# Attention and ternary feed-forward in one kernel: normalisations on GpSimd, head 0's row-max steps inside the token groups, biases as products with ones

## The chip, the cores and the metric

The kernel runs on one core of a Trainium2 chip. Its time is that of the device, in microseconds, as the median over the executions. The core has five engines with a queue each: TensorE (PE: matmuls and transposes, PEld its weight loads), VectorE (DVE), ScalarE (ACT), GpSimd (POOL) and SyncE (SP), which issues most of the DMAs. Each works through its instructions in their order and waits on semaphores.

## The reference

Input x is (2, 2048, 256): two sequences of 2048 tokens with 256 channels, all in float32. Cut to what matters:

```python
xn = (x - mean) / sqrt(var + 1e-5)
# attention: 16 heads of 16 channels, the keys are the queries
z = layernorm(xn) * g + b
q, v = z @ wq.T + bq, z @ wv.T + bv          # k = q
out = softmax(q @ q.T / 4) @ v                # per sequence and head
attn = out @ w_out.T + b_out
# feed-forward with ternary weights: clip(round(w / mean|w|), -1, 1)
h = gelu(xn @ ternary(W1).T + b1)             # 1024 wide
ffn = h @ ternary(W2).T + b2
return x + attn + ffn
```

## The kernel before

**Token groups.** The 4096 tokens are taken in NG = 8 groups of 512, groups 0 to 3 being the first sequence. For a group, VectorE takes the statistics (`stats_of`), GpSimd raises the variances to the power -1/2 (`rsqrt`), and VectorE writes two normalised copies, xn for the feed-forward and zn for the attention, in 8 instructions of 128x256 (`norm`). TensorE transposes both into four PSUM banks. ScalarE and VectorE split the transposed tiles into two float16 parts each (`second_parts`). TensorE then forms half of the values of the group before (`values`), its down projection (`ffn_down`: 64 products of 128x256 into `pf`), the queries of this group in three products of parts, and eight hidden blocks of 128 features. ScalarE applies GELU to each and writes the first float16 part, VectorE the second (`results`, 4 instructions of 128x1024). The down projection of a group thus lies in the TensorE stretch of the next one; that of group 7 comes last. The queries go to DRAM (`q_parts`), from where SyncE loads each head's keys and queries; head 0's are loaded during group 3, once the first sequence is stored.

**Scales.** Before group 0's queries, scales are found that keep the float16 parts in range. ScalarE takes absolute values, TensorE forms sums with them, VectorE adds the biases' part, takes the maximum and derives the scales (`sigma`); the weights are then scaled and split (`scaled`, and a subtraction on VectorE). `ternary` makes the ternary weights from W1 and W2 on VectorE, `out_scale` does for wo what `sigma` does for the others.

**Heads.** There are 32 heads (16 channels x 2 sequences). A head has 32 row-max steps, `a_step`: TensorE writes two products of 128x512 scores into a pair of PSUM banks, and VectorE reduces the 1024 columns to a maximum (`max_step`, L838). There are two such pairs, banks 0 to 3, so step a waits until step a - 2 has been reduced. The groups' transposes use the same four banks, and so wait for all steps given out so far. With a head's maxima complete (`split_max`), they are split into parts, transposed and put below the queries by DMA; then TensorE forms the scores again with the maximum taken off (`b_chunk`, L384), ScalarE takes the exponential (L1046), TensorE multiplies with the values (L367). Head h's exponentials run beside the row-max steps of head h + 1, which are 8 steps ahead (`AHEAD` 2 times `STEPS` 4).

**Order.** All queues are written out by hand. Of head 0's 32 steps, three lie in the hidden blocks of each of groups 4, 5 and 6, after blocks 1, 3 and 5 (`BETWEEN`). In group 7, six lie in the second half of group 6's down projection (`EARLY`) and seven in the hidden blocks. The other ten, and two of head 1, lie in group 7's own down projection. Six more of head 1 follow it, and then the exponentials of head 0 begin. A call `between` in `ffn_down` comes after each four products.

## Time and profile before

| | us |
|---|---|
| median of 3 runs (lowest, highest) | 1461.1 (1459.36, 1463.54) |
| profiled execution | 1464.5 |
| its span | 1462.7 |
| VectorE busy | 1351.0 (92%) |
| TensorE busy | 1396.9 (96%) |
| ScalarE busy | 1243.2 (85%) |
| GpSimd busy | 113.7 (8%) |
| first exponentials' product of head 0 starts at | 240.49 |

TensorE's matmuls are pipelined and their ends are modelled, so its busy time says less than that of the others. The span is that of one profiled execution; the median is over executions without a profile. PEclk is the clock granted to TensorE, as a share of 2.4 GHz. The program's numbers of buffers are left out of names: `w` is w1 or w2, whose buffers later hold the hidden parts and the probabilities; `weight_scratch` holds absolute and scaled weights.

### The profile page before, as it was taken

To read this page: it belongs to the slowest core of one execution; us is meant where nothing else is said; L and a number is where in the kernel's file an instruction comes from. 1 tells how busy PE (TensorE), PEld (TensorE's weight loads), DVE (VectorE), ACT (ScalarE), POOL (GpSimd) and SP (SyncE) were. 2 spreads that over 40 slices of the span, in tenths; PEclk is the share of its full clock that TensorE was granted. 3 is DMA by queue.
4 is the path that set the end of the run, shared out by engine and by line. 5 is a ranking of instruction groups with operands and counts; after the bars stand their busy time and mean duration, and the time that the engine had idled before them with its cause. 6 is when DMAs were issued, how large, how long until landed. Compare 5 with 4: busy or idle time off the path is not lost.

```text
span 1462.7 us, 31753 instructions
## 1 busy us (share of the span) xinstructions
PE 1396.9 (96%) x13166; PEld 445.3 (30%) x13166; DVE 1351.0 (92%) x1430; ACT 1243.2 (85%) x2284; POOL 113.7 (8%) x246
## 2 busy tenths in 40 slices
PE   6899988999999999999999999999999999999999
PEld 4666542222222222222222222222222222222244
DVE  7767789999999999999999999999999999999944
ACT  5564543999999999999999999899999999999975
POOL 2000006000000000000000000000111100001100
PEclk8999998999999999999999999999999999999999
DMA  5012000000000000000000001001212100011122
GB/s 228 15 40 69 30 15 1 28 30 29 29 30 29 30 30 29 26 26 29 29 30 29 30 29 34 30 31 34 59 59 59 59 30 32 31 32 59 38 92 86
DMA packets 28529, 60.65 MB, mean 41 GB/s; under 512 B 6200, under 2 KB 11736, under 8 KB 28130
## 3 DMA queue, kind: packets, MB, share of 16 engines
q1 hardware_dynamic: 27810, 56.99, 11.5%
q8 instruction: 103, 1.69, 0.5%
q10 hardware_dynamic: 576, 1.65, 0.3%
q14 instruction: 40, 0.33, 0.1%
HBM read 41.29 MB, written 16.77 MB: 40 GB/s over the span
## 4 chain that ended last, share of the span: by engine, by line
DVE 54%; PE 37%; ACT 5%; issue 3%; DMA 2%; POOL 0%; SPq 0%; ACTq 0%; DVEq 0%
DVE part_max L838 50%; PE ps L367 13%; PE ps L384 8%; PE ps L330 5%; PE ps L1067 3%; ACT w L1046 3%; PE ps L1136 2%; PE ps L1082 2%; DVE w L830 1%; PE ps L458 1%; ACT w L1017 1%; DMA rows<-in_rows 1%; PE ps L439 1%; PE ps L1108 1%; ACT hidden L1012 1%
## 5 line engine op out<-in xcount | busy, mean ns | idle before, releaser
L838 DVE TENSOR_REDUCE part_max<-ps 128x1 f32<-128x1024 f32 x1024 | 1171.5, 1216 | 16.8 <-PE ps L330 13.8
L1046 ACT ACTIVATE w<-ps 128x512 f32<-128x512 f32 x2048 | 1104.5, 596 | 86.5 <-PE ps L384 50.6
L367 PE MATMUL ps<-w,v_ones 128*32 128x256 f32 (+1 forms) x7440 | 623.8, 407 | 0.4
L384 PE MATMUL ps<-qry,key 50*128 50x512 f16 x1984 | 424.1, 389 | 21.2 <-ACT w L1046 20.7
L330 PE MATMUL ps<-qry,key 48*128 48x512 f16 x2048 | 412.6, 381 | 15.1 <-DVE part_max L838 11.7
L367 PEld LDWEIGHTS ps<-w,v_ones 128*32 128x32 f32 x7440 | 146.6, 108 | 371.1 <-issue 206.8
L384 PEld LDWEIGHTS ps<-qry,key 50*128 50x128 f16 x1984 | 103.9, 93 | 475.3 <-ACT w L1046 443.2
L330 PEld LDWEIGHTS ps<-qry,key 48*128 48x128 f16 x2048 | 102.2, 95 | 46.1 <-DVE part_max L838 33.1
L637 POOL COPY v_ones<-v_all 128x128 f32<-128x128 f32 x64 | 18.6, 291 | 805.8 <-PE ps L367 805.8
L1067 PE MATMUL ps<-w_ternary,w 128*128 128x256 f16 x512 | 62.1, 278 | 6.2 <-DVE w L830 6.2
L1008 ACT ACTIVATE q_split<-ps,sigma_bq 128x512 f16<-128x512 f32 x16 | 11.0, 687 | 66.2 <-PE ps L1082 66.2
L830 DVE SCALAR_TENSOR_TENSOR w<-hidden,hidden_scale,w 128x1024 f16<-128x1024 f32 x32 | 40.9, 1282 | 25.6 <-ACT w L1017 25.5
L1136 PE MATMUL ps<-x,w_ternary 128*128 128x512 f16 x256 | 61.2, 381 | 0.0
L1067 PEld LDWEIGHTS ps<-w_ternary,w 128*128 128x128 f16 x512 | 49.2, 100 | 17.8 <-DVE w L830 7.5
L1012 ACT ACTIVATE hidden<-ps,columns 128x512 f32<-128x512 f32 x64 | 42.2, 680 | 9.5 <-PE ps L1136 8.1
L914 DVE SCALAR_TENSOR_TENSOR resid<-ps,y_unscale,resid 128x512 f32<-128x512 f32 x16 | 11.8, 744 | 30.7 <-PE ps L458 30.6
L1017 ACT ACTIVATE w<-hidden,hidden_scale 128x1024 f16<-128x1024 f32 x32 | 36.7, 1148 | 1.1
L1136 PEld LDWEIGHTS ps<-x,w_ternary 128*128 128x128 f16 x256 | 22.9, 98 | 31.8 <-issue 5.9
L644 POOL TENSOR_TENSOR max_split<-neg_max,shift_unit 128x16 f16<-128x16 f32 x32 | 7.1, 221 | 299.8 <-DVE neg_max L843 299.8
L1082 PE MATMUL ps<-z,wq_parts 128*128 128x512 f16 x96 | 24.6, 411 | 4.9 <-DVE wq_parts L851 4.9
L1082 PE MATMUL ps<-wv_parts,z 128*128 128x256 f16 x192 | 25.2, 285 | 0.0
L1028 ACT ACTIVATE o_evacuated<-ps 128x512 f32<-128x512 f32 x31 | 18.5, 597 | 7.6 <-PE ps L367 7.6
(144 smaller groups left out, 462.4 us busy)
## 6 DMA issues: line engine op xcount, KB each, us to landing
key<-q_parts SPq DMA_DIRECT2D x64, 128.0 KB
qry<-q_parts SPq DMA_DIRECT2D x64, 128.0 KB
o_heads<-o_evacuated SPq DMA_DIRECT2D x31, 256.0 KB, 10.2
resid<-in_x SPq DMA_DIRECT2D x8, 512.0 KB, 13.9
q_parts<-q_split SPq DMA_DIRECT2D x16, 256.0 KB, 2.5
key<-q_parts SPq DMA_DIRECT2D x64, 64.0 KB
qry<-q_parts SPq DMA_DIRECT2D x64, 64.0 KB
out<-resid SPq DMA_DIRECT2D x7, 512.0 KB, 3.6
```

The source lines that it names most:

```text
L330: mm = eng.matmul(pair[:, j * BANK:(j + 1) * BANK], key[v][r:r + ROWS, blk * P:(blk + 1) * P], qry[v][r:r + ROWS, c * BANK:(c + 1) * BANK] ...
L367: mm = eng.matmul(pv[32 * c:32 * c + 2 * D, c0:c1], vst[:, kb, :], prob[kb % 2][:, c * BANK + c0:c * BANK + c1], start=(kb == 0), stop=(kb ...
L384: eng.matmul(ring_bank(v, i, False), key[v][r:r + KROWS, kb * P:(kb + 1) * P], qry[v][r:r + KROWS, c * BANK:(c + 1) * BANK], start=True, s ...
L637: pool.tensor_copy(vst[:, k0:k0 + NBLK // 2, 0:D], v_all[:, ds(b * NBLK + k0, NBLK // 2), ds(hh * D, D)]).then_inc(s_vs, 1)
L830: dve.scalar_tensor_tensor(out=hp[1][:, 2 * i:2 * i + 2, :], in0=hid[:, 2 * i:2 * i + 2, :], scalar=hs[:, 0:1], in1=hp[0][:, 2 * i:2 * i + ...
L838: dve.tensor_reduce(part_max[:, a // 2, a % 2:a % 2 + 1], pa[a % 2], AX.X, ALU.max).then_inc(s_r, 1)
L1012: act.activation(hid[:, f, :], pf[f % 2], ACT.Gelu, scale=1.0 / XS, bias=b1_col[:, f:f + 1]).then_inc(s_g, 1)
L1017: act.activation(hp[0][:, f - 1:f + 1, :], hid[:, f - 1:f + 1, :], ACT.Identity, scale=hs[:, 0:1]).then_inc(s_h1, 1)
L1046: act.activation(prob[kb % 2][:, c * BANK:(c + 1) * BANK], ring_bank(k, i, last), ACT.Exp, scale=exp_scale).then_inc(s_e, 1)
L1067: mm = pe.matmul(pf[t // 2][:, (t % 2) * C:(t % 2 + 1) * C], hp[i][:, f, t * P:(t + 1) * P], w2t[:, f, :], start=(f == 0 and i == 0), stop ...
L1082: mm = pe.matmul(out, rows(k, i, j), cols(k, i, j), start=(m == 0), stop=(m == len(terms) - 1))
L1136: mm = pe.matmul(pf[f % 2], w1t[:, k, f * P:(f + 1) * P], part[:, k, :], start=(k == 0 and i == 0), stop=(k == KC - 1 and i == 1))
```

## The change

- **Norms.** `norm` is a function of the engine now. Group 0's stays on VectorE; those of groups 1 to 7 go to GpSimd, each behind its power. A semaphore of its own (`normed`) tells TensorE, and VectorE, which must not overwrite the means before the norm has read them.
- **GpSimd** also takes the second parts of wq and wv and the float16 cast of the identity; its bias row moves behind the norms.
- **Biases.** bq and bv are loaded as one row on one partition, ahead of w1, instead of with the others on 128 partitions behind it. Their part of the sums comes from three products with a row of ones.
- **wo.** Its absolute values and sum move from group 0 to group 1, its scales to group 1, its scaling on ScalarE to group 2, its second part on VectorE to group 3.
- **Row-max steps.** Five are added in each down projection that lies in groups 4, 5 and 6; six lie in that of group 7's stretch, over three quarters of it, and six in its hidden blocks. All 32 of head 0 and four of head 1 have then been given out. The last four of the eight lie in group 7's own down projection (`REST`), and none follow it. The transpose of head 0's maxima comes ahead of that projection.
- Eight products with ones are added behind group 0's transposes, and an exponential of one column ahead of head 0's, which loads the table.

The diff, cut to its core:

```diff
...
+        row1 = sb("bq_bv", [1, 2 * C])
+        rabs = sb("bq_abs_bv_abs", [1, 2 * C])
...
+        DOWN = 5
+        DOWN_LAST = 6
+        PER_GROUP = DOWN + len(BETWEEN)
+        BEFORE_LAST = (NG - 1 - NG // NB) * PER_GROUP
+        IN_LAST = DOWN_LAST + KF - 2
+        REST = NA + STEPS * AHEAD - BEFORE_LAST - IN_LAST
...
+        def norm(eng, g):
+            x = resid[:, g * TG:(g + 1) * TG, :]
+            wait(eng, s_tr, g)
+            for n, dst in enumerate((xn, zn)):
+                for t in range(TG):
+                    last = eng.tensor_scalar(dst[:, t, :], x[:, t, :], mv[:, t, 0:1], rstd[:, n, t:t + 1],
+                                             ALU.subtract, ALU.mult)
+            last.then_inc(s_nm, 1)
...
+            load_x(1)
             sp.dma_start(w2[:, :], w_2).then_inc(s_w[1], 16)
-            load_x(1)
...
             rsqrt(0)
-            pool.wait_ge(s_row, 16)
-            pool.tensor_tensor(bias_row[:, :], bo_row, b2_row, ALU.add).then_inc(s_row, 1)
+            pool.wait_ge(s_id, 16)
+            pool.tensor_copy(idh[:, :], idf[:, :]).then_inc(s_idh, 1)
+            pool.wait_ge(s_wqs, KC + 1)
+            pool.tensor_tensor(wqp[:, 1, :, :], wqs, wqp[:, 0, :, :], ALU.subtract).then_inc(s_wqp, 1)
+            pool.wait_ge(s_wvs, KC + 1)
+            pool.tensor_tensor(wvp[:, 1, :, :], wvs, wvp[:, 0, :, :], ALU.subtract).then_inc(s_wvp, 1)
             for g in range(1, NG):
                 rsqrt(g)
+                pool.wait_ge(s_rs, g + 1)
+                norm(pool, g)
+            pool.wait_ge(s_out_b, 16)
+            pool.tensor_tensor(bias_row[:, :], bo_row, b2_row, ALU.add).then_inc(s_br, 1)
...
+                wait(dve, s_nm, g)
...
-                dve.wait_ge(s_abs, 3)
-                dve.tensor_tensor(vbound_row[:, :], bound_v, bv_abs[:, :], ALU.add)
-                dve.tensor_tensor(bound_row[:, :], bound_q, bq_abs[:, :], ALU.add).then_inc(s_sg, 1)
+                dve.tensor_reduce(bound[:, 0:2], bound_qv, AX.X, ALU.max)
+                dve.tensor_scalar(bound[:, 2:3], sum_b1, float(C), None, ALU.add).then_inc(s_sg, 1)
...
-                    last = dve.tensor_scalar(bv2[:, j, :], bv_sum[:, :], vsc[:, 0:1], None, ALU.mult)
+                    last = dve.tensor_scalar(bv2[:, j, :], b_wv, vsc[:, 0:1], None, ALU.mult)
...
+                    if g == 1 and i == 2:
+                        out_scale()
...
-            norm(0)
+            dve.wait_ge(s_rs, 1)
+            norm(dve, 0)
             sigma()
             second_parts(0)
-            dve.wait_ge(s_wqs, KC + 1)
-            dve.tensor_tensor(wqp[:, 1, :, :], wqs, wqp[:, 0, :, :], ALU.subtract).then_inc(s_wqp, 1)
             ternary(0, w1, w1t)
             stats_of(1)
-            dve.wait_ge(s_wvs, KC + 1)
-            dve.tensor_tensor(wvp[:, 1, :, :], wvs, wvp[:, 0, :, :], ALU.subtract).then_inc(s_wvp, 1)
             q_split(0)
-            norm(1)
-            dve.wait_ge(s_id, 16)
-            dve.tensor_copy(idh[:, :], idf[:, :]).then_inc(s_idh, 1)
             ternary(1, w2, w2t)
-            out_scale()
             results(0)
-            steps = iter([(0, a) for a in range(NA)] + [(1, a) for a in range(2)])
+            steps = iter([(0, a) for a in range(NA)] + [(1, a) for a in range(STEPS * AHEAD)])
...
-                if g == 1:
+                if g == 3:
                     dve.wait_ge(s_ow, KC + 1)
                     dve.tensor_tensor(wop[:, 1, :, :], wos, wop[:, 0, :, :], ALU.subtract).then_inc(s_op, 1)
-                norm(g + 1)
-                for j in range(2):
-                    add_ffn(g - 1, j)
+                add_ffn(g - 1, 0)
+                if g >= NG // NB:
+                    first_rows(DOWN)
+                add_ffn(g - 1, 1)
                 q_split(g)
                 results(g, first_rows if g >= NG // NB else None)
             g = NG - 1
             second_parts(g)
             value(g - 1, 1)
             add_ffn(g - 1, 0)
-            first_rows(EARLY)
+            first_rows(DOWN_LAST)
             add_ffn(g - 1, 1)
             q_split(g)
             results(g, first_rows)
             value(g, 1)
-            first = EARLY + 2 * (KF // 2 - 1) + (NG - 1 - NG // NB) * len(BETWEEN)
-            first_rows(TG * KF // 4)
-            add_ffn(g, 0)
-            first_rows(NA - first - TG * KF // 4)
-            split_max(0)
-            first_rows(2)
-            add_ffn(g, 1)
+            first_rows(REST)
+            for j in range(2):
+                add_ffn(g, j)
             for h in range(1, NH):
-                for a in range(2 if h == 1 else 0, NA):
+                for a in range(STEPS * AHEAD if h == 1 else 0, NA):
...
+            act.dma_start(row1[:, :], rows[:, 0:2 * C]).then_inc(s_row, 16)
...
+            act.activation(rabs[:, :], row1[:, :], ACT.Abs).then_inc(s_abs, 1)
...
-                    act.wait_ge(s_wo, 16)
-                    act.activation(abso, wo[:, :, :], ACT.Abs).then_inc(s_oa, 1)
                 else:
                     if g == 1:
+                        act.wait_ge(s_wo, 16)
+                        act.activation(abso, wo[:, :, :], ACT.Abs).then_inc(s_oa, 1)
+                    if g == 2:
...
-                pe.wait_ge(s_ln, 4 * g + 4)
+                pe.wait_ge(s_nm, g + 1)
...
                 if g == 1:
                     pe.wait_ge(s_wd, 5)
+                if g == 2:
                     pe.wait_ge(s_od, 1)
-                wait(pe, s_r, max(0, g - NG // NB) * len(BETWEEN))
+                wait(pe, s_r, max(0, g - NG // NB) * PER_GROUP)
...
                     abs_total(0)
+                    warm(WARM // 2)
...
-                        ffn_down(g - 1, t, between_down if t >= TG // 2 else None)
+                        ffn_down(g - 1, t, between_down if t else None)
...
                         abs_total(1)
+                    if g == 1 and f == 1:
                         pe.wait_ge(s_oa, 1)
...
-                    if between and (f in BETWEEN or (g == NG - 1 and f > 1)):
+                    if between and (f > 1 if g == NG - 1 else f in BETWEEN):
...
-            for out, rows, cols in ((bound_q, reach_rep, absq), (bound_v, reach_rep, absv), (b_wv, b_rep, wv)):
+            for out, left, right, bias in ((bound_qv[:, 0, :], reach_rep, absq, rabs[:, 0:C]), (bound_qv[:, 1, :], reach_rep, absv, rabs[:, C:2 * C]),
+                                           (b_wv, b_rep, wv, row1[:, C:2 * C])):
                 for k in range(KC):
-                    pe.matmul(out, rows[:, k, :], cols[:, k, :], start=(k == 0), stop=(k == KC - 1))
+                    pe.matmul(out, left[:, k, :], right[:, k, :], start=(k == 0), stop=False)
+                pe.matmul(out, ones[0:1, :], bias, start=False, stop=True)
...
-            def first_a_early(calls=iter(range(TG * KF // 4))):
-                n = next(calls)
-                if n == 0:
-                    pe.wait_ge(s_z, KC * NG)
-                    pe.wait_ge(s_x2, KC * NG)
-                if n < EARLY:
-                    first_a()
-            for g in range(1, NG - 1):
+            def in_down(g, count):
+                calls = iter(range((TG - 1) * KF // 2))
+                def call():
+                    n = next(calls)
+                    if n == 0:
+                        pe.wait_ge(s_z, KC * (g + 1))
+                        pe.wait_ge(s_x2, KC * (g + 1))
+                    if n % 2 == 0 and n >= (TG - 1) * KF // 2 - 2 * count:
+                        first_a()
+                return call
+            for g in range(1, NG):
+                if g < NG // NB:
+                    group(g)
+                    continue
                 if g == NG // NB:
                     pe.wait_ge(s_pad, 16 * (2 * ROT - 1))
-                group(g, first_a if g >= NG // NB else None)
-            group(NG - 1, first_a, first_a_early)
+                group(g, first_a, in_down(g, DOWN if g < NG - 1 else DOWN_LAST))
+            pe.wait_ge(s_idh, 1)
+            pe.wait_ge(s_vd, 2 * NG - 1)
...
+            max_transpose(pe, 0, 0)
             values(NG - 1, 1)
             pe.wait_ge(s_h2, KF // 2 * NG)
+            rest = iter(range(TG * KF // 2))
+            def rest_a():
+                n = next(rest)
+                if n % 2 and n // 2 < REST:
+                    first_a()
             for t in range(TG):
-                ffn_down(NG - 1, t, first_a)
-            pe.wait_ge(s_idh, 1)
+                ffn_down(NG - 1, t, rest_a)
             pe.wait_ge(s_vd, 2 * NG)
-            max_transpose(pe, 0, 0)
-            for a in range(2, STEPS * AHEAD):
-                a_step(pe, 1, 1, a)
...
```

TensorE in group 5, from the down projection that lies in it to the queries and on. Lines 330 and 333 are the row-max products, 1067 and 1071 the down projection, 1082 and 1086 queries and values, 1136 and 1142 the hidden blocks. Before:

```order
L1067 MATMUL ps<-w_ternary,w 128x256 x64
L1082 MATMUL ps<-z,wq_parts 128x512 x12
L1136 MATMUL ps<-x,w_ternary 128x512 x8
L330 MATMUL ps<-qry,key 128x512 x2
L1136 MATMUL ps<-x,w_ternary 128x512 x8
```

Changed:

```order
L1071 MATMUL ps<-w_ternary,w 128x256 x28
L333 MATMUL ps<-qry,key 128x512 x2
L1071 MATMUL ps<-w_ternary,w 128x256 x8
L333 MATMUL ps<-qry,key 128x512 x2
L1071 MATMUL ps<-w_ternary,w 128x256 x8
L333 MATMUL ps<-qry,key 128x512 x2
L1071 MATMUL ps<-w_ternary,w 128x256 x8
L333 MATMUL ps<-qry,key 128x512 x2
L1071 MATMUL ps<-w_ternary,w 128x256 x8
L333 MATMUL ps<-qry,key 128x512 x2
L1071 MATMUL ps<-w_ternary,w 128x256 x4
L1086 MATMUL ps<-z,wq_parts 128x512 x12
```

The row of 64 products is opened five times for a row-max step; the queries behind it, and the three steps in the hidden blocks, stand as before.

TensorE again, from the values ahead of group 7's own down projection to head 0 (line 351 and 354: the transpose of the maxima; 384 and 387: the exponentials' scores). Before, its beginning (two of twelve steps) and its end:

```order
L1082 MATMUL ps<-wv_parts,z 128x256 x12
L1067 MATMUL ps<-w_ternary,w 128x256 x4
L330 MATMUL ps<-qry,key 128x512 x2
L1067 MATMUL ps<-w_ternary,w 128x256 x4
L330 MATMUL ps<-qry,key 128x512 x2
L1067 MATMUL ps<-w_ternary,w 128x256 x4
```

```order
L1067 MATMUL ps<-w_ternary,w 128x256 x4
L330 MATMUL ps<-qry,key 128x512 x2
L1067 MATMUL ps<-w_ternary,w 128x256 x16
L351 MATMUL ps<-ident_f,max_split 32x128
L330 MATMUL ps<-qry,key 128x512 x12
L384 MATMUL ps<-qry,key 128x512 x2
L330 MATMUL ps<-qry,key 128x512 x2
```

Changed, the whole of it:

```order
L354 MATMUL ps<-ident_f,max_split 32x128
L1086 MATMUL ps<-wv_parts,z 128x256 x12
L1071 MATMUL ps<-w_ternary,w 128x256 x8
L333 MATMUL ps<-qry,key 128x512 x2
L1071 MATMUL ps<-w_ternary,w 128x256 x8
L333 MATMUL ps<-qry,key 128x512 x2
L1071 MATMUL ps<-w_ternary,w 128x256 x8
L333 MATMUL ps<-qry,key 128x512 x2
L1071 MATMUL ps<-w_ternary,w 128x256 x8
L333 MATMUL ps<-qry,key 128x512 x2
L1071 MATMUL ps<-w_ternary,w 128x256 x32
L387 MATMUL ps<-qry,key 128x512 x2
```

Eight of twelve steps have left the projection, and the six that stood behind the transpose are gone.

GpSimd, behind its first constants, with what each waits for. Before:

```order
L620 TENSOR_TENSOR rstd<-var_eps,minus_half 128x8 [waits ln_dve]
L624 TENSOR_TENSOR bias_row<-rows 128x256 [waits rows_loaded]
L620 TENSOR_TENSOR rstd<-var_eps,minus_half 128x8 [waits ln_dve] x7
L637 COPY v_ones<-v_all 128x8x16 [waits v_done]
L637 COPY v_ones<-v_all 128x8x16
L644 TENSOR_TENSOR max_split<-neg_max,shift_unit 128x16 [waits max_dve]
```

Changed, to the second norm:

```order
L633 TENSOR_TENSOR rstd<-var_eps,minus_half 128x8 [waits ln_dve]
L637 CAST ident_f<-ident_f 128x128 [waits ident_loaded]
L639 TENSOR_TENSOR wq_parts<-weight_scratch,wq_parts 128x512 [waits wq_scaled]
L641 TENSOR_TENSOR wv_parts<-weight_scratch,wv_parts 128x512 [waits wv_scaled]
L633 TENSOR_TENSOR rstd<-var_eps,minus_half 128x8 [waits ln_dve]
L500 TENSOR_SCALAR xn<-resid,mean_var,rstd 128x256 [waits transposed,ln_pool]
L500 TENSOR_SCALAR xn<-resid,mean_var,rstd 128x256 x3
L500 TENSOR_SCALAR zn<-resid,mean_var,rstd 128x256 x4
L633 TENSOR_TENSOR rstd<-var_eps,minus_half 128x8 [waits ln_dve]
L500 TENSOR_SCALAR xn<-resid,mean_var,rstd 128x256 [waits transposed,ln_pool]
L500 TENSOR_SCALAR xn<-resid,mean_var,rstd 128x256 x3
```

Each later power now stands behind the norm of the group before, and the staging of head 0's values behind all seven norms.

## Rows read from the trace of the kernel before

**Rows 1.** The page: span, and the costliest group of lines (busy, mean ns, idle before).

```profile
span 1462.7 us, 31753 instructions
...
L838 DVE TENSOR_REDUCE part_max<-ps 128x1 f32<-128x1024 f32 x1024 | 1171.5, 1216 | 16.8 <-PE ps L330 13.8
```

**Rows 2.** Stages: window, length, PE, PEld, DVE, ACT, POOL busy, PEclk, DMA share, GB/s.

```profile
44.00:53.00 9.00, 8.88 (x65) 7.23 (x66) 8.29 (x27) 0.00 (x0) 1.64 (x1) 0.81 0.01 2
68.00:112.00 44.00, 42.59 (x297) 28.50 (x296) 31.80 (x67) 25.58 (x37) 3.27 (x2) 1.00 0.12 39
219.00:241.00 22.00, 15.47 (x101) 6.84 (x99) 21.93 (x22) 1.55 (x2) 8.38 (x15) 0.97 0.00 1
241.00:254.00 13.00, 12.90 (x72) 2.28 (x70) 9.66 (x10) 8.00 (x15) 13.00 (x20) 0.52 0.01 1
```

**Rows 3.** Timeline of the start: start, length, engine, line, shapes, idle before.

```profile
12.18 1.07 PE L1108 MATMUL ps<-ident_f,xn 128*128 128x128 f32 x8
...
15.34 0.42 DVE L776 TENSOR_TENSOR v_bound_row<-ps,bv_abs 128x256 f32<-128x256 f32 x1 [3.57 <-ACT bq_abs L973]
...
17.03 1.06 ACT L986 ACTIVATE x<-ps 128x512 f16<-128x512 f32 x2
...
22.44 5.30 PE L1082 MATMUL ps<-z,wq_parts 128*128 128x512 f16 x12 [4.88 <-DVE wq_parts L851]
...
28.92 0.69 ACT L1012 ACTIVATE hidden<-ps,columns 128x512 f32<-128x512 f32 x1 [0.46 <-PE ps L1136]
...
38.60 3.68 DVE L830 SCALAR_TENSOR_TENSOR w<-hidden,hidden_scale,w 128x1024 f16<-128x1024 f32 x3
...
38.69 1.15 ACT L1017 ACTIVATE w<-hidden,hidden_scale 128x1024 f16<-128x1024 f32 x1
```

**Rows 4.** Chain of waits: start and length of five down projections on TensorE.

```profile
44.12 8.83 PE ps L1067 x64
...
67.80 7.16 PE ps L1067 x64
...
89.86 7.16 PE ps L1067 x64
...
138.50 6.99 PE ps L1067 x64
...
164.85 6.99 PE ps L1067 x64
```

**Rows 5.** Timeline of TensorE in group 4, of VectorE in group 5.

```profile
123.40 0.39 PE L330 MATMUL ps<-qry,key 48*128 48x512 f16 x2
...
133.59 1.58 PE L1108 MATMUL ps<-ident_f,xn 128*128 128x128 f32 x8 [2.35 <-DVE part_max L838]
...
142.37 0.68 DVE L752 TENSOR_TENSOR v_all<-ps,scaled_bv 128x512 f32<-128x512 f32 x1
```

**Rows 6.** GpSimd: timeline of two instructions, then groups of lines.

```profile
28.49 2.02 POOL L620 TENSOR_TENSOR rstd<-var_eps,minus_half 128x8 f32<-128x8 f32 x1 [13.22 <-DVE var_eps L714]
...
48.55 1.64 POOL L620 TENSOR_TENSOR rstd<-var_eps,minus_half 128x8 f32<-128x8 f32 x1 [18.03 <-DVE var_eps L714]
...
L631 POOL TENSOR_TENSOR resid<-resid,bias_row 128x256 f32<-128x256 f32 x32 | 21.9, 725 | 0.0
...
L664 POOL TENSOR_TENSOR hidden<-below_half,hidden 128x512 f16<-128x512 f32 x8 | 9.3, 1159 | 0.6
L662 POOL CAST hidden<-below_half 128x512 f16<-128x512 f32 x8 | 4.9, 609 | 0.5
```

**Rows 7.** Timeline of the last group and of the way into head 0.

```profile
193.40 0.39 PE L330 MATMUL ps<-qry,key 48*128 48x512 f16 x2
...
194.26 0.39 PE L330 MATMUL ps<-qry,key 48*128 48x512 f16 x2
...
218.59 0.61 PE L1067 MATMUL ps<-w_ternary,w 128*128 128x256 f16 x4 [1.12 <-DVE w L830]
...
235.43 11.40 DVE L838 TENSOR_REDUCE part_max<-ps 128x1 f32<-128x1024 f32 x10
```

99 lines of the change are left out of this document (43 added, 56 removed).

## The prediction

> **What bounds the kernel now.** I read the page first, then the table of stages, then the chain of waits with the timeline beside it for the first 275 us. The page [rows 1] gives VectorE's row-max reduction 1171.5 us of a span of 1462.7 us, with 16.8 us of idle time before its 1024 instructions: once the heads run, VectorE sets the pace. The change leaves a head alone, so it can only act ahead of a fixed point in head 0. I take the ninth row-max step of head 1. Both kernels have 40 steps behind them there, and everything after it is the same on every engine. VectorE's ten reductions from 235.43 begin with the third step of head 1 and take 1.14 each, so the ninth begins at 235.43 + 6 x 1.13 = 242.2 us [rows 7].
>
> Ahead of it lie eight token groups. In the plain groups TensorE is busy 42.59 of 44 us [rows 2], and one down projection follows the other after 89.86 - 67.80 = 22.06 us [rows 4]: TensorE, then ScalarE's last GELUs and VectorE's last hidden part. Groups 4 to 6 carry three row-max steps each and take 164.85 - 138.50 = 26.35 [rows 4]. From the last group's down projection on, VectorE is full (21.93 of 22 us) and TensorE waits for it (15.47) [rows 2].
>
> The sum is made against the profiled execution: 1464.5 us, span 1462.7. The median of the runs is 1461.1, and I put the difference on it.
>
> **The start, down to group 0's down projection (at 44.12).** VectorE's sigma chain begins at 15.34 after 3.57 of idle, behind two absolute values whose bias rows come in behind w1 [rows 3]. The small load now goes ahead of w1, and the three added products with ones run ahead of the transposes. The sums ended as the transposes began, at 12.18 [rows 3]; three more of 256 float32 columns cost about 0.5 each by their neighbours' pace, and the new absolute value of 512 columns delays them by about 0.5. So the sums end at 14.1, the transposes at 16.1, and ScalarE's copies start at 16.2, not 17.03 [rows 3]: 0.8 earlier. The first float16 part of wq then comes 0.8 earlier, GpSimd's subtraction (1.16 for this form) stands where VectorE's 0.68 stood, but VectorE's was queued behind its x and z parts. GpSimd's ends at about 20.9, so the q products start 1.5 ahead of their 22.44 [rows 3, 6], and the first GELU at 27.4 instead of 28.92.
>
> ScalarE needs from there to 38.69 + 1.15 = 39.84, that is 10.9 [rows 3]; without the wo product between the second and third hidden block, 0.6 less. Its last part is there at 37.7. Before, VectorE was late, not ScalarE: it took up the first three hidden parts only at 38.60 [rows 3]. The change takes from its queue ahead of them eight normalisations, two subtractions, a cast, the out-scale steps and a wait for GpSimd, some 7 us together. Now it needs 1.3 after ScalarE's last, and the down projection starts at 39.1: **-5.0**. The three cover each other: if only VectorE's queue improved, ScalarE's chain would still hold it at 41.2, which is -2.9. TensorE has no 2.9 us hole ahead of it any more, so the projection takes 7.16 rather than 8.83 [rows 4] at the granted clock of 0.81 there [rows 2]: **-1.7** (bounds -1.7 and 0). In group 1 the wo product (1.1 on TensorE) lies between hidden blocks where ScalarE has about 0.2 to spare: **+0.9**. The scale steps and casts of wo, moved to groups 1 to 3, lie in VectorE's and ScalarE's waits for TensorE: 0.
>
> **Norms on GpSimd.** No row shows this form there. Nearest are the two-input 128x256 addition at 725 ns and the one-input 128x512 cast at 609 ns [rows 6], so I take 0.5 each, 4 us for eight, between 0.3 and 1.3. In a plain group statistics end 4 us into the period, the power takes 1.64 [rows 6], and the transposes wait 18 us in: hidden up to 1.5 us each. In group 0 there are about 7 us for the eight, hidden up to 0.85 each. That VectorE is relieved of 2.8 us in a plain group is worth 0, because TensorE and ScalarE set the 22.06.
>
> **Five more steps in each down projection of groups 4 to 6.** A step costs TensorE 194.26 - 193.40 = 0.86 less the 0.45 of four projection products, so about 0.42 [rows 7]. Five are 2.1. VectorE must end the parts, the statistics and the values of the group (142.37 + 0.68, that is 4.55 after the projection's start at 138.50 [rows 4, 5]) and one residual addition before its first reduction, which ends at 6.35; the third step waits for that where it would have gone at 5.8. So 0.6 is lost, and 2.7 a group: **+8.1** for three (bounds 6.3, no stall, and 12). The steps inside the hidden blocks keep their order, and with it TensorE's 2.35 us wait before each group's transposes [rows 5]. The very first step is 3.1 us into group 3's projection (115.1) and needs head 0's queries and keys; before, it came at 123.40 and did not wait for them [rows 5]. Their loads are issued from 104 on: **+1.0**, between 0 and 8.3.
>
> **The last group and the way into head 0.** Six steps were in its second half before and are spread now: +0.8 for a stall on the third; the head's final maximum now falls in VectorE's full stretch: +0.2. Together **+1.0**. Group 7's own down projection starts at 218.59 [rows 7], and here the gain is. It holds four steps instead of twelve, and six outside are gone. TensorE needs 7.16 + 4 x 0.42 = 8.85; VectorE, at 1.13 a step, is not late. Two residual additions close it, the second at 228.3; the exponentials' products start, and the ninth step of head 1 comes two products and a step later, at 229.2 instead of 242.2: **-13.0** (bounds -11.5 and -13.6). The max rows' transpose and load, now ahead of the projection, are covered by it.
>
> **The clock in head 0.** From 241 to 254 the granted clock was 0.52, the low level of 1.2 GHz, and VectorE worked 9.66 of 13.0 us [rows 2]. It fell after TensorE had waited through five steps for VectorE at the end of the last group. That stretch is gone; TensorE now works 8.85 us through just before. I take **-3.0**, between 0 and the 3.3 that VectorE stood idle.
>
> **Contention.** GpSimd's power took 2.02 us beside a VectorE subtraction of two SBUF tensors, and 1.64 elsewhere [rows 6]. Its norms of group 1 now run beside VectorE's ternary steps, its bias additions (32 of 725 ns, 22 us, no longer beside row maxima alone) beside the hidden parts of group 7: **+1.0**, between 0 and 5. The Trainium skill, "SBUF — State Buffer", the reading of its diagram, has a rule against this change: the pair of ports that VectorE and GpSimd share is an exclusive lock for a whole instruction, taken by VectorE operations in a two-port mode or with two SBUF inputs. By that rule alone each meeting costs up to a whole instruction; the 0.38 us of the power agrees in direction.
>
> **Sum.** -5.0 - 1.7 + 0.9 + 8.1 + 1.0 + 1.0 - 13.0 - 3.0 + 1.0 = -10.7 us. 1461.1 - 10.7 = **1450.4 us**.
>
> **Rivals.**
> *A, half of it* (GpSimd and VectorE hinder each other). In group 0 eight norms of 0.5 and five VectorE instructions of 1.3 to 2.35 us take turns, so the norms end near 40 rather than 33, and the first projection at 42: +3. In group 7 three hidden parts wait up to 0.7 each: +2 over all. With the middle of the last term taken back: 1461.1 - 10.7 + 4 = 1454.4. For it speaks the 2.02; against it the reductions beside 22 us of GpSimd additions, still 1.13. This is where the skill's lock leads, worked out from these rows.
> *B, the clock stays low* in head 0 and after group 0: 3.0 + 1.7 come back, 1455.1. For it: TensorE still waits 2.35 in groups 4 to 6 and again for the two additions.
> *C, slower*: GpSimd's norm becomes the bound of every group. The place is the transposes' wait for the normed tiles. It decides from 1.5 us an instruction; each 0.1 more costs at most 0.8 in six groups, 4.8 in all, and the 10.7 are used up at 1.75: at 2.0 us, 1461.1 - 10.7 + 24 = 1474. Against it: the worst elementwise row there, with twice the columns, is below 1.3. The skill's "GPSIMD Engine Reference", section "Engine selection", advises VectorE for elementwise work and calls GpSimd about two times slower with two inputs, roughly line rate with one; that would leave it far from 1.5.
> *D, head 0's loads are late*: the first step stalls by 6 and TensorE's clock drops: 1450.4 + 6 = 1456.5.
> *E, the steps ride free*: no stall in the projections, no contention, full clock: 1446.
>
> **Chances.** Forecast 0.45, A 0.18, B 0.13, D 0.06, E 0.13, C and what I did not see 0.05. Runs spread by about 0.15% to either side, so 0.3% (4.4 us) is about what can be told from no change. The range takes the forecast, A, B and E: 1443 to 1457. Faster by over 4.4 us means below 1456.7: 0.86, with part of D beyond it; same 0.09; slower 0.05.
>
> **What would show it.** The first down projection near 39 and 7.2 long; the distance between down projections of groups 4 to 6 near 29; the first step of head 0 without a wait above 2; a granted clock of 1.0 over the 13 us after the exponentials begin, which begin near 233 (240.5 before); and heads of the same length as before. It is wrong if the transposes of any group wait for GpSimd, or if the heads themselves change.

## The result, and the profile after

| us | before | after |
|---|---|---|
| median of 7 runs (lowest, highest) | 1461.1 (1457.36, 1463.54) | 1471.31 (1467.09, 1473.16) |
| profiled execution, its span | 1464.5, 1462.7 | 1471.57, 1469.7 |

The ratio is 1.0066, 95% interval 1.0049 to 1.0084: slower by two thirds of a per cent, where 1450.4 us was forecast, between 1443 and 1457. Runs of one kernel lie 5 to 15 us apart where there are seven or more, and the higher the mean granted clock of a run, the shorter it is (1467.42 us at 0.991, 1471.57 at 0.986). Medians are compared below, and profiled executions only stage by stage. The medians are 10.2 us apart and the profiled executions 7.0: that of the kernel before lies 3.4 above its own median.

Everything behind the heads' start is as before. The page of the changed kernel answers to [rows 1]:

```profile
span 1469.7 us, 31804 instructions
...
L846 DVE TENSOR_REDUCE part_max<-ps 128x1 f32<-128x1024 f32 x1024 | 1171.6, 1213 | 18.5 <-PE ps L333 15.2
```

So the 7 us arose ahead of head 1's exponentials. The table sets the starts of the down projections on TensorE beside each other. The last row is head 1's final maximum, which both kernels reach with the same work behind them and some 1189.6 us ahead.

| | before | after | difference | this interval | forecast |
|---|---|---|---|---|---|
| group 0's projection | 44.12 | 50.01 | +5.9 | +5.9 | -5.0 |
| group 1's | 67.80 | 72.72 | +4.9 | -1.0 | -0.8 |
| group 3's | 111.93 | 116.74 | +4.8 | 0 | 0 |
| group 4's | 138.34 | 152.54 | +14.2 | +9.4 | +3.7 |
| group 5's | 164.65 | 180.17 | +15.5 | +1.3 | +2.7 |
| group 6's | 189.37 | 209.46 | +20.1 | +4.6 | +2.7 |
| group 7's | 218.59 | 241.40 | +22.8 | +2.7 | +1.0 |
| head 1's final maximum | 273.19 | 280.01 | +6.8 | -16.0 | -16.0 |

The windows of the changed kernel that answer to [rows 2], with one on the first row-max steps and one behind the exponentials' start (columns as there):

```profile
44.00:53.00 9.00, 7.86 (x56) 7.31 (x57) 3.44 (x7) 2.69 (x5) 1.09 (x1) 0.73 0.00 0
68.00:112.00 44.00, 42.55 (x298) 28.73 (x296) 28.85 (x55) 27.13 (x40) 23.23 (x18) 1.00 0.09 28
120.00:134.00 14.00, 9.73 (x52) 4.95 (x51) 8.16 (x16) 0.00 (x0) 11.32 (x9) 0.76 0.19 65
219.00:241.00 22.00, 17.61 (x94) 8.18 (x93) 17.72 (x18) 12.88 (x17) 10.03 (x13) 0.90 0.08 26
251.00:264.00 13.00, 11.65 (x106) 2.84 (x108) 12.04 (x11) 10.86 (x21) 5.38 (x8) 1.00 0.01 1
```

In the plain groups TensorE is as full as it was, though GpSimd now works 23 us in 44. From 44 to 53 it is not: its transposes begin only at 45.14. The chain of waits of the changed kernel says why (start, length, what; [rows 4] began with the same projection at 44.12):

```profile
29.11 1.65 POOL rstd L633
30.77 0.09 issue
30.86 8.82 POOL xn L500 x4
39.68 5.42 POOL zn L500 x4
45.10 0.04 issue
45.14 3.68 PE ps L1113 x16
48.82 1.36 PE ps L1086 x12
50.18 6.99 PE ps L1071 x64
```

Eight normalisations of group 1 take 14.24 us on GpSimd. The timeline of VectorE in the same stretch (start, length, line, shapes, idle before) shows that it had its hidden parts done by 40.4, 9.6 us before the projection, and what it ran beside the norms:

```profile
30.70 1.29 DVE L713 TENSOR_SCALAR below_half<-w,nhalf 128x2048 f32<-128x2048 f32 x1
32.02 2.53 DVE L715 SCALAR_TENSOR_TENSOR w_ternary<-w,half,below_half 128x2048 f16<-128x2048 f32 x1
34.65 3.93 DVE L838 SCALAR_TENSOR_TENSOR w<-hidden,hidden_scale,w 128x1024 f16<-128x1024 f32 x3
38.51 0.68 DVE L764 TENSOR_TENSOR v_all<-ps,scaled_bv 128x512 f32<-128x512 f32 x1
39.11 1.27 DVE L838 SCALAR_TENSOR_TENSOR w<-hidden,hidden_scale,w 128x1024 f16<-128x1024 f32 x1
```

TensorE's timeline at the first row-max steps of the changed kernel, and ahead of its last projection:

```profile
124.45 0.61 PE L333 MATMUL ps<-qry,key 48*128 48x512 f16 x2 [4.27 <-DMA qry<-q_parts]
124.99 1.89 PE L1071 MATMUL ps<-w_ternary,w 128*128 128x256 f16 x8
...
131.48 1.05 PE L1071 MATMUL ps<-w_ternary,w 128*128 128x256 f16 x8
...
147.83 1.94 PE L1113 MATMUL ps<-ident_f,xn 128*128 128x128 f32 x8 [2.35 <-DVE part_max L846]
...
238.66 0.27 PE L354 MATMUL ps<-ident_f,max_split 128*32 128x128 f16 x1 [3.78 <-issue]
238.86 2.74 PE L1086 MATMUL ps<-wv_parts,z 128*128 128x256 f16 x12
```

The first step waits 4.27 us for head 0's queries, and eight products behind it take 1.89 us instead of 1.05: the granted clock was at its low level, 1.2 GHz. The last row, twelve products that take 1.47 us elsewhere, shows the same ahead of the last projection.

### The profile page after: what moved, and what is told of

It reads as the page before. It is cut to its first block, busy times and chain, and to the rows that moved or that the text cites. A ratio compares the mean times of both kernels' runs of the same rounds, so it can differ in the third digit from the quotient of the medians.

```text
span 1469.7 us, 31804 instructions
## 1 busy us (share of the span) xinstructions
PE 1400.5 (95%) x13188; PEld 450.7 (31%) x13188; DVE 1334.3 (91%) x1367; ACT 1242.9 (85%) x2284; POOL 194.0 (13%) x305
## 4 chain that ended last, share of the span: by engine, by line
DVE 51%; PE 38%; ACT 4%; issue 3%; DMA 1%; POOL 1%; SPq 0%; ACTq 0%; DVEq 0%; POOLq 0%
DVE part_max L846 49%; PE ps L370 12%; PE ps L387 8%; PE ps L333 5%; PE ps L1071 3%; ACT w L1049 3%; PE ps L1086 2%; PE ps L1142 2%; PE ps L461 2%; PE ps L442 1%; PE ps L1113 1%; DMA qry<-q_parts 1%; PE ps L431 1%; ACT w L1020 1%; DVE w L838 1%
## 5 line engine op out<-in xcount | busy, mean ns | idle before, releaser
L500 POOL TENSOR_SCALAR xn<-resid,mean_var,rstd 128x256 f32<-128x256 f32 x28 | 37.9, 1366 | 0.7
L500 POOL TENSOR_SCALAR zn<-resid,mean_var,rstd 128x256 f32<-128x256 f32 x28 | 35.4, 1280 | 0.0
L988 ACT ACTIVATE x<-ps 128x512 f16<-128x512 f32 x16 | 8.6, 590 | 23.7 <-PE ps L1113 23.7
## 6 DMA issues: line engine op xcount, KB each, us to landing
o_heads<-o_evacuated SPq DMA_DIRECT2D x31, 256.0 KB, 10.2
```

Source lines behind the costliest of these rows:

```text
L500: last = eng.tensor_scalar(dst[:, t, :], x[:, t, :], mv[:, t, 0:1], rstd[:, n, t:t + 1], ALU.subtract, ALU.mult)
```

## The experiments

Lines of a diff are against the changed kernel unless said otherwise. Intervals are those between down projections, as in the table.

**1. Norms of group 1 back on VectorE.** Theory: GpSimd's norms of group 1 cost the start.

```diff
+                if g > 1:
+                    pool.wait_ge(s_rs, g + 1)
+                    norm(pool, g)
 ...
+            dve.wait_ge(s_rs, 2)
+            norm(dve, 1)
             ternary(1, w2, w2t)
```

> Only the norm of group 1 goes back to VectorE, into its old place between the query split and the second ternary weight; groups 2 to 7 stay on GpSimd. Theory L (the late norm of group 1 alone loses the start: GpSimd needs 1.22 us an instruction and was shut out by VectorE's instructions on two SBUF inputs): the first down projection starts at about 43.4 instead of 50.2, everything behind it moves by as much, so about 6.8 us less than the changed kernel, near 1464.5. Rival M (the longer instruction hurts in every group): the distances between later down projections shrink only with all norms moved, and this kernel gains at most the start's idle time of a few us, under 4. Rival W (the start was lost to ScalarE or to the clock, not to the norm): the first down projection stays above 48.

Measured: 1466.05 us (12 runs), ratio 1.0029 (1.0009 to 1.005). The first projection:

```profile
42.07 9.75 PE L1074 MATMUL ps<-w_ternary,w 128*128 128x256 f16 x64 [4.25 <-DVE w L839]
```

It starts 7.9 us earlier than in the changed kernel and lasts 2.6 longer (9.75 for 7.15): TensorE idled 4.25 us before it, and the granted clock fell; experiment 11 fills that wait. Some 5.3 us remain, and the medians differ by as much (1471.31 and 1466.05).

**2. VectorE held back until the norms are done.** Why 14.24 us for eight? Either that is this form's own pace, or the two engines shut each other out.

```diff
+            dve.wait_ge(s_nm, 2)
             ternary(1, w2, w2t)
```

> VectorE waits for GpSimd's norm of group 1 before it begins the second ternary weight, so the eight norm instructions run with VectorE idle. Theory K (the two engines shut each other out): the eight take 8 x 1.22 = 9.8 us instead of 14.2, and the first four 4.9 instead of 8.8. Rival F (the first instructions of this kind are slow for another reason, as the first use of their code): the first four still take over 8 us. The down projection then comes behind VectorE, at about 51 us, so the total stays within 2 us of the changed kernel.

Measured: 1474.73 us (one run). GpSimd's timeline:

```profile
31.62 4.83 POOL L500 TENSOR_SCALAR xn<-resid,mean_var,rstd 128x256 f32<-128x256 f32 x4
36.43 4.82 POOL L500 TENSOR_SCALAR zn<-resid,mean_var,rstd 128x256 f32<-128x256 f32 x4
```

With VectorE idle the eight take 9.65 us, 1.2 each; beside its two-input and wide instructions 14.24. So 4.6 us come from VectorE at work beside them, and 9.65 are the engine's own pace. The Trainium skill, "SBUF — State Buffer", "Who interferes with whom", says that a GpSimd instruction that reads SBUF and VectorE work in a two-port mode or with two SBUF inputs shut each other out, whichever is issued first holding the ports for its whole instruction. The trace agrees in direction, and shows who pays: GpSimd 4.6 us, VectorE 0.4 (2.53 for 2.35 and 3.93 for 3.68, as in experiment 1). The lock itself no row shows. The Trainium skill's "GPSIMD Engine Reference", "Engine selection", calls one-input work there roughly line rate; the trace disagrees, with 1.2 us where VectorE takes 0.34 (1.38 for four, in experiment 11).

**3. No steps in group 3's projection, six in those of groups 4 and 5, seven instead of four in the last.** If the steps' place before the loads have landed is the cost, this should take it away.

```diff
-        DOWN = 5
+        DOWN = {4: 0, 5: 6, 6: 6}
```

> No row-max step in the down projection that lies in group 4, six instead of five in those of groups 5 and 6, six in group 7's and seven instead of four in the last. Theory D (head 0's queries arrive too late for steps at 120 us): the 4.3 us wait for the queries and the half-speed stretch behind it go, group 3's down projection takes 7.2 us instead of 16.6, that is 9.4 less; each step moved costs 0.4 to 0.9 elsewhere (two in groups 5 and 6: 1.5 together, three in the last projection: 1.3), so about 6.5 us less than the changed kernel, near 1465. Rival S (the steps themselves are the cost, wherever they stand): at most 2 us less.

Measured: 1468.47 us (6 runs), ratio 1.0071 (1.0047 to 1.0094). The interval of group 3 fell from 35.8 to 24.9, as expected; the next two rose from 27.6 and 29.3 to 30.6 each, and the way from the last projection to head 1's final maximum from 38.6 to 43.4. So 10.9 us won by then are paid for with 9.1: the loads' wait is real, but spreading the steps otherwise gave most of it back.

**4. The last values ahead of the maximum's transpose.** After group 7's hidden blocks TensorE waits 3.78 us ahead of the transpose of the max rows, and the values stand behind it.

```diff
+            values(NG - 1, 1)
             pe.wait_ge(s_idh, 1)
             pe.wait_ge(s_vd, 2 * NG - 1)
             max_transpose(pe, 0, 0)
-            values(NG - 1, 1)
```

> Behind group 7's hidden blocks TensorE forms the second half of the values first, and then waits for the first half's evacuation and transposes the maxima of head 0; the changed kernel has these the other way round. Theory V (the transpose's wait held up the values, which cost 2.7 us at the low clock on the path): the last down projection starts right after VectorE's last hidden part, 1.3 us earlier, and runs its first products faster, so 1.5 to 3 us less than the changed kernel. Rival: VectorE's last hidden part is what the down projection waits for anyway, and nothing changes (within 0.7).

Measured: 1474.6 us (4 runs), ratio 1.0101 (1.008 to 1.0121): no gain. Its windows:

```profile
231.00:237.00 6.00, 2.59 (x18) 1.38 (x16) 6.00 (x6) 2.83 (x4) 6.00 (x7) 0.89 0.00 0
237.00:241.00 4.00, 3.83 (x17) 2.17 (x18) 1.94 (x3) 0.76 (x2) 4.00 (x6) 0.50 0.02 4
```

The projection now starts right behind VectorE's last hidden part, not 1.3 us later, but at a granted clock of 0.50, and the interval is 32.3 us, not 31.9. The order alone was not the cause: TensorE's wait stands ahead of the projection now, and the clock falls there.

**5 and 6. Head 0 loaded alone first**, with group 1's norms on VectorE (5) and without (6). Head 0's eight loads share the queue with those of heads 1 and 2: does that make them late, or do they take that long by themselves?

```diff
-            for h in range(ROT):
+            load_head(0, 0)
+            sp.wait_ge(s_ld[0], 128)
+            for h in range(1, ROT):
```

> Group 1's norm on VectorE, and SyncE waits until head 0's eight loads have landed before it issues those of heads 1 and 2. Theory Q (the loads of three heads share the queues, so head 0's land late behind or beside the others): the first row-max step, 120 us in, waits under 2 us instead of 4.3 and TensorE's clock does not fall behind it; group 3's projection to group 4's comes down from 32.9 to about 28, and the total lies 4 to 5 us under that of the kernel with only the norm moved, near 1461. Rival R (head 0's eight loads take 11 us by themselves): the wait stays 4.3 and the total does not change.

> The changed kernel with the one edit that heads 1 and 2 are loaded only after head 0 has landed. Theory Q: distance from group 3's down projection to group 4's 28 us instead of 35.8 (here the low clock took more behind the wait); total about 7 less. Rival R: 33 to 36 as before.

Measured: 1463.83 us (12 runs), ratio 1.0015 (0.9999 to 1.0031), and 1469.92 (one run). The first step of the fifth kernel:

```profile
122.53 0.39 PE L333 MATMUL ps<-qry,key 48*128 48x512 f16 x2 [2.94 <-DMA qry<-q_parts]
```

The wait falls from 4.3 to 2.9 only (2.75 in the sixth, whose interval is 30.2 instead of 35.8). The eight loads, all issued by 112.95, let TensorE go 9.6 us later with nothing else in the queue, and 11.0 later in the changed kernel with sixteen others behind them. So company costs 1.4 us and the eight loads by themselves the rest; experiment 10 asks whether it is their size.

The fifth kernel's profiled execution shows something else. Its code up to the first projection is that of the first kernel, and yet that projection starts at 47.75, not 42.07. The granted clock fell in the sums ahead of group 0's transposes; four products of the sums, in the first kernel and in the fifth:

```profile
10.48 1.13 PE L1172 MATMUL ps<-weight_scratch,reach_rep 128*128 128x256 f32 x4
...
10.59 2.00 PE L1174 MATMUL ps<-weight_scratch,reach_rep 128*128 128x256 f32 x4
```

Twelve kernels here have the new order of the sums, and in the profiled executions of six of them, the changed one too, group 0's transposes ran at the low level. The queries' products then start 1.0 to 2.2 us later than in the other six, in the fifth kernel 5.7. In the two kernels with the old order the transposes ran at the high level (1.07 us for eight). One execution of each can't say how often either happens, or whether the order has to do with it, but the start in a single profile is no sharper than that.

**7. All norms on VectorE, the steps as in the change.** Are GpSimd's norms worth anything?

```diff
-                pool.wait_ge(s_rs, g + 1)
-                norm(pool, g)
 ...
+                dve.wait_ge(s_rs, g + 2)
+                norm(dve, g + 1)
                 add_ffn(g - 1, 0)
```

> All norms on VectorE again, each where it stood before the change, everything else as changed. Against the kernel with only group 1's norm moved. Theory H (from group 2 on GpSimd's norm hides wholly, and what it takes off VectorE counts only where row-max steps stand in the down projection): plain groups 22.0 us as they are; in groups 4 to 6 VectorE's first reduction comes 2.8 us later, the third step waits for it, and each of these groups takes about 2.8 us more, 8 in all. Rival N (VectorE's norm was free there too): distances of groups 4 to 6 unchanged within 0.5 us.

Measured: 1476.08 us (one run). TensorE in group 4's projection:

```profile
156.32 0.61 PE L333 MATMUL ps<-qry,key 48*128 48x512 f16 x2 [4.57 <-DVE part_max L844]
```

The plain groups take 22.0 us either way, but groups 4 and 5 take 33.9 and 34.2, not 27.6 and 29.3. VectorE comes to its reductions only behind eight norms. The interval of group 3, where the loads' wait is the longer one, stays at 32.8. Norms on GpSimd are what makes room for the added steps; at 6.3 and 4.9 us a group, lower clock included (0.90 granted in both), the effect is about twice what I expected.

**8. The fifth kernel, with two of the last steps moved into TensorE's wait ahead of the last projection**, and the values first, as in 4.

```diff
+            values(NG - 1, 1)
+            first_a()
+            first_a()
             pe.wait_ge(s_idh, 1)
```

> On top of the norm and the loads: the last values stand ahead of the transpose of the maxima again, and two of the last four row-max steps stand between them, where TensorE otherwise waits for VectorE. Theory G (in the swapped order alone the time came back as low clock, because TensorE stood still for 3.6 us before the projection): with TensorE at work in that gap the projection runs at full clock; from group 6's projection to the first exponentials' product it takes about 40.5 us instead of 42.6, and the total is 2 us under that of the kernel without this edit, near 1459. Rival: VectorE is the bound of that stretch, and its work is the same: less than 0.7 us.

Measured: 1463.6 us (12 runs), ratio 1.0014 (0.9997 to 1.0031): the last interval is 30.7 instead of 31.7, the total the same as in 5.

**9. The first kernel with the steps where they were before the change.** What is the new schedule of steps worth?

```diff
+        DOWN = {4: 0, 5: 0, 6: 0}
 ...
-                if n % 2 and n // 2 < REST:
+                if n < REST - 6:
                     first_a()
```

Six more steps stand behind the last projection again, and VectorE's order goes with it.

> The changed kernel with group 1's norm on VectorE and the row-max steps as before the change (three in the hidden blocks of groups 4 to 6, six in group 7's down projection stretch, six and not seven in its hidden blocks, thirteen in its own down projection, six behind). Theory P (the step schedule brings 16 us at the end, and costs 1.4, 3 and 1 in the groups and 6 at the late loads, so about 5 net with the loads as they are; the start and the norms on GpSimd bring 1 to 2): distances of groups 3 to 7 26.4, 26.3, 24.7 and 29.3 as before the change, the end 54.6, and the total 4 us above the kernel with only the norm moved. Rival O (spreading the steps costs as much as it brings): the total lies within 1.5 us of it.

Measured: 1463.74 us (12 runs), ratio 1.0015 (1.0001 to 1.0028), no slower than the first kernel with the new schedule. The profiled executions of the two agree: the 15.3 us that the new schedule wins behind the start of the last projection (38.6 against 53.9 to head 1's final maximum) are paid for with 15.9 in the four intervals ahead (121.8 against 105.8), of which the late loads have some 5.

**10. The eighth kernel, with three quarters of head 0 loaded before the last quarter is stored.**

```diff
+            load_first(0, L - BANK, s_early)
+            store_q(NG // NB - 1)
             sp.wait_ge(s_qs, 16 * KC * NG // NB)
+            load_first(L - BANK, L, s_ld[0])
```

> On the kernel with the norm moved and the gap filled: three quarters of head 0's queries and keys (the tokens of groups 0 to 2) are loaded before group 3's are stored, and only the last quarter behind it. Theory Q2 (the eight DMAs take 10 to 11 us because of their size, four times what the last quarter is): the first row-max step waits under 0.5 us instead of 2.9 to 4.3, TensorE's clock stays up, distance from group 3's projection to group 4's 27.5 to 28.5 instead of 33.0, and the total 4 to 5 us less, near 1459. Rival R2 (the wait is issue and latency of eight DMAs, not their bytes): the wait falls by less than 1.5 us.

Measured: 1460.65 us (12 runs), ratio 0.9998 (0.9981 to 1.0016). TensorE at the first step, and at the transposes of the next group:

```profile
116.54 0.39 PE L334 MATMUL ps<-qry,key 48*128 48x512 f16 x2
...
137.93 1.91 PE L1129 MATMUL ps<-ident_f,xn 128*128 128x128 f32 x8 [2.35 <-DVE part_max L860]
```

The first step no longer waits. The last eight loads, a quarter of the size, were all issued 3.4 us ahead of the projection, as in experiment 5 (3.2), and were there at most 6.8 us later, where the whole ones took 9.6: it was their size, not when they could be issued. Group 3's interval is 29.5, 1.7 of it transposes at the low clock.

**11. The tenth kernel, with sixteen products with ones ahead of group 0's projection**, to hold the clock. The profile shows each of them as two, so 32.

```diff
+                    if g == 1:
+                        pe.wait_ge(s_g, KF)
+                        warm(WARM)
                     pe.wait_ge(s_h2, KF // 2 * g)
```

> The last kernel, with sixteen products with ones (32 passes of 128 columns, 3.4 us at full clock) behind group 1's values, where TensorE waits 4.3 us for VectorE's last hidden part of group 0. Theory T (that wait is what drops the clock in the first down projection, which takes 25.3 to the next one instead of 22.7): 22.7 and 2.5 us less in total, near 1456.5. Rival: the products push the down projection back by as much as the clock brings.

Measured: 1455.96 us (12 runs), ratio 0.9963 (0.9948 to 0.9979), the one version that beats the kernel before. Its timeline on TensorE:

```profile
37.76 3.74 PE L1179 MATMUL ps<-ones 128*128 128x128 f32 x32
42.17 7.16 PE L1087 MATMUL ps<-w_ternary,w 128*128 128x256 f16 x64 [0.67 <-DVE w L852]
...
133.68 1.06 PE L1129 MATMUL ps<-ident_f,xn 128*128 128x128 f32 x8 [2.35 <-DVE part_max L860]
```

The projection takes 7.16 us, where the tenth kernel's took 9.80, and group 3's interval is 27.8, its transposes at full clock.

**12. The same products in the kernel before** (diff against that one). Whose gain is it?

```diff
+                    if g == 1:
+                        pe.wait_ge(s_g, KF)
+                        for _ in range(WARM):
+                            pe.matmul(pf[1][:, 0:P], ones[:, :], ones[:, :], start=True, stop=True)
                     pe.wait_ge(s_h2, KF // 2 * g)
```

> The kernel before, with 32 more products with ones on TensorE between group 0's last GELU and its down projection; the rest as before. The question is whose gain the 4.7 us of the last version were. Theory S (the products give what they gave there to any kernel): there they took the first projection from 9.80 to 7.16 us and the median down by 4.7 us; here 8.83 goes to 7.2 and the median comes 4 to 5 us below the kernel before, about 1457. Rival T (they pay only where TensorE has a long hole): before, TensorE stands idle from 41.2 to 44.1, that is 2.9 us; 32 products of 0.117 take 3.7, so the projection starts 0.8 later and is 1.7 shorter: 1460, or no difference that can be told, and what the last version is ahead by belongs to the change's own edits.

Measured: 1460.51 us (12 runs), ratio 1.0001 (0.999 to 1.0012). This is what rival T said:

```profile
40.97 3.74 PE L1120 MATMUL ps<-ones 128*128 128x128 f32 x32
44.54 7.15 PE L1067 MATMUL ps<-w_ternary,w 128*128 128x256 f16 x64
```

The projection is 1.7 us shorter and starts 0.4 later, and the median doesn't move by more than the interval's 0.1%.

## Why the prediction was wrong, by its own steps

The forecast for the profiled execution was -10.7 us, and +7.0 came: 17.7 apart. By the medians it was -10.7 and +10.2; the 3.2 between the two are in no row below, and some 2 of them may be what the paragraph on the end closes with.

**"Norms on GpSimd" and its contention failed, and with them the start: 10.9 us of the miss.** VectorE's last hidden part ended at 40.4, so 9.6 us of them are the norms' and 1.3 lie ahead of them. I took 0.5 us a norm, between 0.3 and 1.3, by the 609 ns of a cast of twice the columns and the 725 ns of an addition [rows 6]. Alone it is 1.21 (experiment 2), inside the bounds and far from the value taken. Group 0's stretch hides 0.85 each, by the prediction's own working; so even alone they were 0.36 x 8 = 2.9 us too long there (3.3 by the rows of this execution: the eight would have ended at 40.5, and the transposes and values take 3.2 at the high clock before the projection). VectorE's work beside them adds 4.6 (experiment 2). That is the term "Contention", which named just this meeting and put +1.0 on it, between 0 and 5. TensorE, idle for 9.32 us ahead of them, then does the transposes at the low clock: 3.68 us for sixteen, where [rows 3] have 1.07 for eight; that is 1.7 more. The three make the 9.6.

Experiment 1 puts the projection at 42.07 with group 1's norms (2.7 us) back in VectorE's queue, that is, as an estimate, at 39.4 without them: what the prediction said of the rest of the start, 39.1, was near. The changed kernel's own 40.4 has the low clock of group 0's transposes in it (1.80 and 1.92 us for eight each), which the prediction did not see coming: it kept their pace of before. The way there was forecast less exactly, with the queries' products at 22.83 (21.77 in experiment 1) for a forecast of 20.9. Rival A had this mechanism at +3 for the start, with 0.5 a norm; rival C had the long norm, but placed it in the plain groups, where 1.2 stays below its 1.5 and costs nothing, and asked nothing of group 0, where it decides from 0.85. So the step that failed is the pair of prices, of the norm on GpSimd and of its meeting with VectorE, in the one stretch that could not hide them.

**Head 0's loads: +1.0 forecast, about 6.** The wait is 4.27 us, within the bound of 8.3. What I left out is behind it: some 2 us of low clock in the products that follow (1.89 for 1.05 twice, 1.51 once, and 0.61 for 0.39 in three steps). Rival D had it as it came, with +6, and I gave it 0.06. Experiment 10 removes the wait, and the eleventh kernel, with neither wait nor low clock there, has 27.84 where the changed kernel has 35.8; the rest of these 8.0 us are 1.7 of transposes at the low clock, which the kernel before has too.

**Five steps a projection: right.** At full clock a group with them takes 27.63 and one without 24.9 (experiment 9; 24.72 before), so 2.8 against 2.7. The intervals +1.3 and +4.6 differ from it by 1.5 and 1.8, one each way, because the sixteen transposes behind the 2.35 us wait run at the low clock in some groups and not in others, in both kernels. Over the three groups this cancels: 3 x 2.8 and 6.3 of the loads make 14.7 of the 15.3 measured.

**The last interval: +1.0 forecast, +2.7.** The values stand behind the max rows' transpose and its 3.78 us of waiting, and ran at the low clock (2.74 us for twelve). Experiments 4 and 8 say that the order alone is not it: each gain of about 1 us came with low clock or left the total alone. The third step waits 1.54 us for VectorE here, where the prediction had 0.8. How the 1.7 divides is open.

**The end: -16.0 for -13.0 and -3.0, the first right, the second in part luck.** From the last projection's start to head 1's ninth row-max reduction it is 11.3 us instead of 23.6, that is -12.3, within the bounds. The exponentials start 10.7 us behind the projection instead of 21.9. From the ninth reduction to the final maximum it is 27.3 instead of 31.0, -3.7, and the 13 us after the exponentials' start have a granted clock of 1.00 where [rows 2] have 0.52. But the clock there is no fixed property of the old schedule: it was 0.69 and 0.66 in the profiled executions of experiments 9 and 12, which have the old end (28.9 and 29.2 us), and 0.87 in the tenth kernel's, which has the new one (28.9 us). So some 2 of the 3.7 us belong to the one execution of the kernel before that was profiled, which is also slower than its median.

**Contention beyond the start: next to nothing.** Plain groups keep 22.0 us. Two hidden parts of group 7 take 1.51 and 1.60 us instead of 1.28 beside the bias additions. What the term costs at the start is in the first row, so its 1.0 is taken off here. The misses, row by row of the table, are 10.9 - 0.2 + 6.2 (groups 3 to 5 together) + 1.7, and -1.0 for this term: 17.6 of the 17.7.

**What the repaired kernel owes to what.** 1466 with group 1's norms on VectorE, 1463.8 with head 0 loaded alone, 1460.7 with three quarters loaded early, 1456.0 with the clock held. Only the last of these steps lies between intervals that don't meet. Experiment 9 shows that moving the steps brought nothing while head 0's loads were late. With the loads early it may: the eleventh kernel takes 8.0 us more than the ninth in the four intervals ahead of the last projection, and 14.4 less behind it (39.5 against 53.9). That is an estimate from two executions; no run has the old steps with the other repairs. Experiment 12 shows that the products alone bring nothing either. They paid where TensorE waited 4.25 us ahead of the projection and not where it waited 2.94; that the longer wait is the reason is a reading of these two cases, not shown. In runs at the same mean clock of 0.991 the kernel before takes 1459 to 1461 us, the changed one 1467.4 and the eleventh 1459.6: its lead goes with the clock, which was 0.991 to 0.996 in 11 of its 12 runs. Of the 8.3 us between the profiled executions of 10 and 11 the first projection has 2.6. Another 1.6 arise ahead of the added products, where the tenth's transposes of group 0 ran at the low clock, and twice 1.7 in later transposes. Whether the clock held there because of the products or by chance was not settled.

## What to carry to other kernels

Before a step moves to another engine, compare its duration there with the shortest stretch it must fit into, not with the steady one: 1.2 us a norm was free in six groups and, beside VectorE's work, put the projection 9.6 us late in the one where 0.85 was hidden; taking it back gained 5.3 net. Where neither trace nor row has the form, price it at the upper bound for that stretch. A wait on TensorE can cost more than its length, when the work behind it runs at the lower clock (4.27 us of waiting and 2 more behind it at head 0's first step), and a shortened start may return as idle time ahead of the next long projection unless something keeps TensorE busy. And where executions of one kernel differ by more than the effect, one profile of each is no comparison: look for the same stretch in the profiles of several variants that share it.

## What the runs showed of the hardware

- A GpSimd subtract-and-multiply with two per-partition scalars of 128x256 float32 takes 1.2 us (experiment 2), more than an addition of two such tiles at 0.73 to 0.79 (means in the two kernels), and 3.5 times VectorE's 0.34. Beside two-input and wide VectorE instructions four took 8.82, that is 2.2 each.
- Eight loads of a head's rows, of 64 and 128 KB, issued over 4.5 us, are there 9.6 us after the last is issued when alone in the queue (experiment 5), and 11.0 after with sixteen more behind them; eight of a quarter of the size in at most 6.8 (experiment 10).
- Sixteen transposes of 128x128 float32 take some 2.0 us at the high clock and 3.7 at the low one. Behind a wait of TensorE of 2.35 us they ran at either, at 3.6 in group 4 of the changed kernel and at 2.0 in that of the eleventh.
- The same sums at the start, at the same point of the program, ran at the high clock in one kernel's profiled execution (1.13 us) and at the low one in another's (2.00).
